# States gathered behind the scores into the banks of values and of y, summed by one running sum out of PSUM, and the share put behind the own values

## The chip, the core and the metric

The kernel runs on one core of a Trainium2 chip. The metric is device time in microseconds: the median of three runs of the kernel before is 128.42 us (127.86 to 129.88).

## What is computed

Eight batches of 512 tokens with 128 features. Each is normalised, goes through retention attention with 8 heads of 16 features in blocks of 64 tokens, and through a feed-forward layer of 512 hidden features with squared relu, whose weights are rounded to -1, 0 and 1 times a scale. Cut to what matters:

```python
qs, ks, vs = map(to_chunks, (q, k, v))          # blocks of 64 tokens
def step(S, x):
    qc, kc, vc = x
    attn = jnp.einsum('bhid,bhjd->bhij', qc, kc) * D
    o_intra = jnp.einsum('bhij,bhje->bhie', attn, vc)
    o_inter = jnp.einsum('bhid,bhde->bhie', qc * decay_q[None, :, :, None], S)
    S_new = decay_s[None, :, None, None] * S + jnp.einsum('bhjd,bhje->bhde', kc * decay_k[None, :, :, None], vc)
    return (S_new, o_intra + o_inter)
...
h = _bitlinear(x, w_fc) + gate * (x @ v.T @ fast_b.T @ u.T)
r = jnp.maximum(h, 0.0)
return _bitlinear(r * r, w_proj)
...
xn = _layernorm(x, axis=-1)
x = x + attention(xn) + ffn(xn)
```

## The kernel before

Everything is written out by hand: each engine has its own program, and semaphores with counts tie them together. The batches go through a prologue (the first batch's projections and hidden layer, and all weights), a loop of three rounds with two bodies each (batches 1 to 6), and a tail for the last batch. A body of index b carries three batches at once: it computes hidden layers and attention of b, finishes b - 1 and normalises and projects b + 1.

Full-width products are split in three terms (`three_terms`, L659, L660, L663) or are single products of 512 columns. The attention is made of small tiles of the 128x128 array:

- `score` (L705): 32 products of 32 rows and 64 columns, into the four banks of `ps_score`. `mask_scores` (L516, DVE) multiplies each bank by the causal mask into `scores`.
- `gather_states` (L720): 28 products of 64 rows and 32 columns, k transposed times v for each block of 64 tokens. They go into two banks of `ps_score` (numbers 2 and 3) and so must wait until the masks of these banks are done.
- `own_values` (L735): 64 products of 64 rows and 32 columns, the part of the output that comes from the tokens of the block itself, into banks 0 and 1.
- `carry` (L747), called the share here: 28 products of 32 rows and 32 columns, the part of the earlier blocks. Its weights are the sums of the states over all blocks before. It adds to the banks of `own_values`. `o_done` then lets ACT round the sum (`high_o`, L360, `o_hi`), and DVE takes what is left (`low_o`, L538, `o_lo`).

The sums of the states take DVE four instructions: `take_states` (L524) masks them into `sums_of[0]`, and `add_states` (L532) adds with distances of 1, 2 and 4 blocks. Each waits for the one before.

In a body TensorE does, in this order: hidden layers 0 and 1, the second product and the share of the batch before, hidden layers 2 and 3, the turn of xn (`turn_xn`, L668, four transposes into `ps_turn`), the scores, the output product of the batch before, q, k and values by token (`project_vk`, two banks, `ps_turn` and `ps_y`), the states and own values. DVE in a body: statistics of b + 1, `take_states` and `add_states` of b - 1 with the variance between them, four steps of the inverse root, normalising (L491, four instructions), `low_o`, `low_xn` (L497), two masks, `finish` (L544), `decay_q` (L501), two masks, `take_v` twice. ACT takes relu, squares (`take_square`) and their rounded copies (`high_square`). POOL subtracts the copies (`low_square`, L300) and spreads q over pairs of heads (`spread_q`, L305).

## Time and profile before

| | us |
|---|---|
| median of three runs | 128.42 |
| profiled execution, its own time | 129.01 |
| its span, first to last instruction | 127.04 |
| TensorE busy | 117.0 |
| DVE busy | 99.2 |
| ACT busy | 78.7 |
| POOL busy | 64.0 |
| prologue, to the first product of the loop | 24.89 |
| bodies of batches 1 to 6 | 15.02, 15.26, then 52.71 for four |
| tail, from the last batch's first product | 19.16 |

The span is what the trace shows, and the execution lasts 1.97 us longer. A row of the timeline has the start, the time from the first to the last instruction of the row, the engine, the line and the shapes. A matmul's end is modelled and lies behind the start of its successor, so distances between starts tell the pace. TensorE takes a product of 32-bit numbers that aren't rounded in two passes, so 28 products are x56 in the trace.

### The profile page before, as it was taken

The numbers are of one execution on the slowest core, as the hardware profiler recorded it, in microseconds if no ns is written. First come the engines' busy times: TensorE is split into PE (matmuls) and PEld (weight loads), VectorE is DVE, ScalarE is ACT, GpSimd is POOL, SyncE is SP. The second block draws the span as 40 slices with busy tenths as digits, with TensorE's granted clock in tenths as the row PEclk, the third lists the DMA queues.
The fourth block names the chain that finished last, engine by engine and source line by source line (L and its number), as shares of the span: only waits on it lengthen the run. The fifth ranks groups of instructions, "written<-read, shape, count | busy, mean of one in ns | idle before, by whom it ended". The sixth has DMA issues, their size and how long they took to land.

```text
span 127.0 us, 6564 instructions
## 1 busy us (share of the span) xinstructions
PE 117.0 (92%) x2860; PEld 92.8 (73%) x2860; DVE 99.2 (78%) x261; ACT 78.7 (62%) x158; POOL 64.0 (50%) x60
## 2 busy tenths in 40 slices
PE   4979999988999999499999999999999999499991
PEld 4425869856688778377788778878897889377890
DVE  0788795489799969858699979896999799729832
ACT  3265669967871897227972897188738774382910
POOL 7099803984439161923439252916193529544400
PEclk9999999999999999999999999999999999999998
DMA  3849920000023000400023001300020002000202
GB/s 105 296 149 320 389 92 34 0 3 5 8 90 81 5 0 23 145 7 0 0 92 74 0 0 53 112 0 0 0 83 0 0 0 83 0 5 0 88 5 83
DMA packets 3357, 7.71 MB, mean 61 GB/s; under 512 B 384, under 2 KB 896, under 8 KB 3216
## 3 DMA queue, kind: packets, MB, share of 16 engines
q1 hardware_dynamic: 2880, 7.01, 16.3%
q10 hardware_dynamic: 464, 0.50, 1.2%
q8 instruction: 11, 0.18, 0.6%
q14 instruction: 2, 0.02, 0.0%
HBM read 5.42 MB, written 2.10 MB: 59 GB/s over the span
## 4 chain that ended last, share of the span: by engine, by line
PE 80%; DVE 10%; issue 4%; ACT 2%; POOL 1%; DVEq 0%; POOLq 0%
PE ps_work L659 10%; PE ps_score L735 8%; PE ps_work L663 7%; PE ps_work L660 7%; PE ps_score L705 6%; PE ps_score L747 5%; PE ps_score L781 5%; PE ps_y L761 4%; PE ps_y L762 4%; PE ps_score L720 3%; DVE sums_of L532 3%; PE ps_turn L668 3%; PE ps_y L765 2%; DVE xn L491 2%; PE ps_turn L692 1%
## 5 line engine op out<-in xcount | busy, mean ns | idle before, releaser
L300 POOL TENSOR_TENSOR sq_lo<-square,sq_hi 128x512 fp32r<-128x512 f32 x31 | 39.8, 1295 | 36.2 <-ACT sq_hi L356 36.2
L347 ACT ACTIVATE square<-ps_work 128x512 f32<-128x512 f32 x32 | 19.1, 596 | 23.1 <-PE ps_work L663 22.6
L516 DVE TENSOR_TENSOR scores<-ps_score,cst 128x512 f32<-128x512 f32 x32 | 20.3, 682 | 1.6 <-PE ps_score L705 1.6
L305 POOL TENSOR_TENSOR q_pair<-q_dec,cst 128x1024 f32<-128x1024 f32 x7 | 13.3, 1894 | 15.9 <-DVE q_dec L501 15.9
L356 ACT ACTIVATE sq_hi<-square 128x512 fp32r<-128x512 f32 x32 | 20.1, 627 | 0.1
L352 ACT ACTIVATE square<-square 128x512 f32<-128x512 f32 x32 | 18.9, 630 | 0.1
L491 DVE TENSOR_SCALAR xn<-x_in,mean_var,rstd 128x128 f32<-128x128 f32 x32 | 14.9, 528 | 0.3
L659 PE MATMUL ps_work<-xn_hi,w_hi 128*128 128x512 f32 x32 | 14.3, 447 | 0.4 <-issue 0.4
L735 PE MATMUL ps_score<-scores,v_pad 64*32 64x64 f32 x1024 | 12.5, 225 | 1.6 <-issue 1.6
L663 PE MATMUL ps_work<-xn_lo,w_hi 128*128 128x512 f32 x32 | 12.6, 394 | 0.0
L660 PE MATMUL ps_work<-xn_hi,w_lo 128*128 128x512 f32 x32 | 12.6, 393 | 0.0
L735 PEld LDWEIGHTS ps_score<-scores,v_pad 64*32 64x32 f32 x1024 | 11.0, 105 | 2.1 <-issue 1.8
L532 DVE TENSOR_TENSOR sums_of<-sums_of 128x224 f32<-128x224 f32 x24 | 12.0, 502 | 0.6
L761 PE MATMUL ps_y<-sq_hi,w 128*128 128x512 f32 x28 | 11.2, 400 | 0.5 <-POOL sq_lo L300 0.5
L762 PE MATMUL ps_y<-sq_lo,w 128*128 128x512 f32 x28 | 11.0, 392 | 0.0
L497 DVE TENSOR_TENSOR xn_lo<-ps_turn,xn_hi 128x512 fp32r<-128x512 f32 x8 | 5.5, 692 | 6.6 <-ACT xn_hi L334 6.6
L458 DVE BATCH_NORM_STATS2 stats<-x_in 128x6 f32<-128x128 f32 x32 | 6.9, 279 | 4.6 <-DMA x_in<-x_tok 4.0
L747 PEld LDWEIGHTS ps_score<-q_dec,sums_of 32*32 32x32 f32 x448 | 6.6, 105 | 4.8 <-issue 4.8
L747 PE MATMUL ps_score<-q_dec,sums_of 32*32 32x64 f32 x448 | 7.9, 216 | 2.1 <-DVE sums_of L532 2.1
L705 PE MATMUL ps_score<-q_pair,k_feat 32*64 32x128 f32 x512 | 9.7, 278 | 0.0
L705 PEld LDWEIGHTS ps_score<-q_pair,k_feat 32*64 32x64 f32 x512 | 7.7, 130 | 1.5 <-DVE o_lo L538 0.9
L659 PEld LDWEIGHTS ps_work<-xn_hi,w_hi 128*128 128x128 f32 x32 | 6.0, 187 | 3.1 <-issue 0.7
(123 smaller groups left out, 238.6 us busy)
## 6 DMA issues: line engine op xcount, KB each, us to landing
x_in<-x_tok SPq DMA_DIRECT2D x8, 256.0 KB, 3.4
resid<-x_feat SPq DMA_DIRECT2D x1, 2048.0 KB, 7.7
out_feat<-resid SPq DMA_DIRECT2D x7, 256.0 KB
po_in<-ffn_weights SPq DMA_DIRECT2D x1, 320.0 KB, 3.2
fc_in<-ffn_weights SPq DMA_DIRECT2D x1, 256.0 KB, 3.7
q_table<-q_decay SPq DMA_DIRECT2D x1, 256.0 KB, 3.5
wqvk<-qvk_weights ACTq DMA_DIRECT2D x1, 192.0 KB, 3.9
cst<-const ACTq DMA_DIRECT2D x1, 129.0 KB, 3.9
```

The costliest lines, as they stand in the source:

```text
L300: nc.gpsimd.tensor_tensor(sq_lo[p][:, f, :], square[p][:, f, :], sq_hi[p][:, f, :].bitcast(F32), ALU.subtract).then_inc(lo_ready, 1)
L347: nc.scalar.activation(square[b.parity][:, f, :], ps_work[f % 2][:], ACT.Relu).then_inc(relu_ready, 1)
L352: nc.scalar.activation(sq, sq, ACT.Square).then_inc(square_ready, 1)
L356: nc.scalar.activation(sq_hi[b.parity][:, f, :], square[b.parity][:, f, :], ACT.Copy).then_inc(hi_ready, 1)
L491: ins = nc.vector.tensor_scalar(xn[:, t, :], x_in[b.parity][:, t, :], mean_var[:, t, 0:1], rstd[:, t:t + 1], ALU.subtract, ALU.mult)
L516: nc.vector.tensor_tensor(scores[:, g].rearrange("p t s i -> p (t s) i"), ps_score[:, g].rearrange("p (a i) -> p a i", i=BLK), causal.unsq ...
L659: mm(out, w_hi, x_hi, start=True, stop=False)
L660: mm(out, w_lo, x_hi, start=False, stop=False)
L663: return mm(out, w_hi, x_lo, start=False, stop=True)
L705: ins = mm(ps_score[r * BLK:(r + 1) * BLK, g, t * P:(t + 1) * P], k_feat[b.parity][rows, toks], q_pair[b.parity][rows, :, toks], start=Tru ...
L735: mm(ps_score[g * GW:(g + 1) * GW, r, t * BLK:(t + 1) * BLK], v_pad[b.parity][rows, t, g, s * GW:(s + 1) * GW], scores[rows, g, t, s, :], ...
L747: ins = mm(ps_score[rows, r, t * BLK:(t + 1) * BLK], sums_of[3][rows, PAD + blk - 1, :], q_dec[b.parity][rows, blk * BLK:(blk + 1) * BLK], ...
```

## The change

The states are gathered right behind the scores, into the first columns of `ps_turn` and `ps_y`, now two halves of one tensor `ps_both`. They don't wait for a mask any more, but the turn of xn, which writes `ps_turn`, waits until `take_states` has read them. `take_states` of batch b now stands in the body of b. It writes the masked states back to PSUM (bank 2 of `ps_score`, whose scores have been masked by then), with the blocks innermost. One instruction on DVE, a running sum (`tensor_tensor_scan`), multiplies by `restart` (0 at the start of each run of 8 blocks, 1 elsewhere) and adds. The share reads its weights out of `state_sums` with a step of 8 elements, and stands behind the own values of the same batch. The second product stands as a whole behind the turn. DVE and ACT work a body ahead on the statistics: the variance of b + 2 is at the end of the body of b, which makes their last bodies stand outside the loop. POOL zeroes no paddings but sets up `restart`, and does all four subtractions before it spreads q. The last of them in the tail has moved from DVE to POOL. The 32-row products that TensorE runs in the prologue to pass the time are now `place_program`: 12, 27 (behind the first turn) and 7 (between own values and share of the first batch), and 22 in the tail in place of 6.

```diff
+        state_sums = sb("state_sums", [P, GW * NBLK])
+        restart = sb("restart", [P, GW * NBLK])
...
+        ps_both = pb("ps_both", [P, ROWS, SEQ])
+        ps_turn, ps_y = ps_both[:, 0, :], ps_both[:, 1, :]
+        w1_bank = ps_score[:, NG - 1, :]
+        masked_states = ps_score[:, ROWS, 0:GW * NBLK]
...
             def take_states(b):
 
+                dve.wait_ge(scores_ready, b.count(NG, 1))
                 dve.wait_ge(state_done, b.count(1, 1))
                 nc.vector.tensor_tensor(
-                    sums_of[0][:, PAD:].rearrange("p (t r) e -> p t r e", r=ROWS),
-                    ps_score[:, ROWS:2 * ROWS, 0:NT * GW].rearrange("p r (t e) -> p t r e", e=GW),
...
-            def add_states(b, k):
-                dve.wait_ge(state_step, b.count(3, k + 1))
...
+                    masked_states.rearrange("p (e t r) -> p r t e", t=NT, r=ROWS),
+                    ps_both[:, :, 0:NT * GW].rearrange("p r (t e) -> p r t e", e=GW),
+                    pair_mask.unsqueeze(1).unsqueeze(1).broadcast_to([P, ROWS, NT, GW]),
+                    ALU.mult).then_inc(states_taken, 1)
+
+            def sum_states(b):
+                dve.wait_ge(states_taken, b.count(1, 1))
+                nc.vector.tensor_tensor_scan(state_sums[:], restart[:], masked_states, 0.0, ALU.mult,
+                                             ALU.add).then_inc(state_ready, 1)
...
-            def turn_xn(b):
+            def turn_xn(b, before=None):
                 pe.wait_ge(xn_ready, b.count(1, 1))
+                if before is not None:
+
+                    pe.wait_ge(states_taken, before.count(1, 1))
...
-                pe.wait_ge(scores_ready, b.count(NG, ROWS))
+                pe.wait_ge(v_ready, b.count(2, 2))
...
-                            ins = mm(ps_score[g * GW:(g + 1) * GW, ROWS + r, t * GW:(t + 1) * GW],
+                            ins = mm(ps_both[g * GW:(g + 1) * GW, r, t * GW:(t + 1) * GW],
...
-                        ins = mm(ps_score[rows, r, t * BLK:(t + 1) * BLK], sums_of[3][rows, PAD + blk - 1, :],
+                        ins = mm(ps_score[rows, r, t * BLK:(t + 1) * BLK], state_sums[rows, blk - 1:GW * NBLK:NBLK],
...
+            def place_program(n, bank, data):
+
+
+                for k in range(n):
+                    rows = slice(k % NG * GW, (k % NG + 1) * GW)
+                    mm(bank[rows, 0:BLK], data[rows, 0:GW], data[rows, 0:BLK], start=True, stop=True,
+                       skip_group_check=True)
...
+            place_program(27, ps_score[:, 0, :], ident)
...
+            own_values(first)
+            place_program(7, ps_score[:, NG - 1, :], ident)
+            carry(first)
+
+            def hidden_and_scores(b):
 
                 pe.wait_ge(q_ready, b.count(1, 1))
                 hidden(b, 0)
                 pe.wait_ge(k_ready, b.count(1, 1))
                 hidden(b, 1)
...
+                pe.wait_ge(o_lo_ready, b.count(1, 0))
+                score(b)
+                gather_states(b)
                 hidden(b, 2)
                 hidden(b, 3)
...
+                turn_xn(after, b)
+                second_product(before, ps_y, range(NF))
                 output_product(before, ps_y)
                 project_q(after, b)
                 project_k(after, b)
                 project_vk(after, 0)
                 project_vk(after, 1)
-                gather_states(b)
                 own_values(b)
+                carry(b)
...
+            hidden_and_scores(last)
+            pe.wait_ge(states_taken, last.count(1, 1))
+            second_product(before, ps_y, range(NF))
             output_product(before, ps_y)
...
+            pe.wait_ge(scores_ready, last.count(NG, NG))
+            pe.wait_ge(state_ready, last.count(1, 1))
+            place_program(22, ps_score[:, NG - 1, :], ident)
             own_values(last)
             carry(last)
...
+            for f in range(NF):
+                last_second(f)
```

On TensorE, in the second body of the loop before (the names stand for tiles without their numbers; REGISTER_ALU and ISA rows set up waits), the share stands between the second product and hidden layer 2:

```order
L761 MATMUL ps_y<-sq_hi,w 128x512
L762 MATMUL ps_y<-sq_lo,w 128x512
L747 MATMUL ps_score<-q_dec,sums_of 32x64 x28
L754 ISA
L659 MATMUL ps_work<-xn_hi,w_hi 128x512
```

In the same body of the changed kernel, scores and states stand there, behind hidden layer 1:

```order
L679 MATMUL ps_work<-xn_hi,w_lo 128x512
L682 MATMUL ps_work<-xn_lo,w_hi 128x512
L719 ISA
L725 MATMUL ps_score<-q_pair,k_feat 64x128 x32
L740 MATMUL ps_both<-v_pad,k_tok 32x32 x28
L774 ISA
L678 MATMUL ps_work<-xn_hi,w_hi 128x512
```

So scores and states have become neighbours ahead of hidden layers 2 and 3, and the turn comes behind both.

At the end of the same body TensorE had, behind the last product of the values by token:

```order
L694 MATMUL ps_y<-wqvk_hi,xn_lo 128x2x128
L720 MATMUL ps_score<-v_pad,k_tok 32x32 x28
L735 MATMUL ps_score<-scores,v_pad 32x64 x64
L83 REGISTER_ALU
L83 COMPARE_AND_BRANCH
```

and has now:

```order
L714 MATMUL ps_both<-wqvk_hi,xn_lo 128x2x128
L755 MATMUL ps_score<-scores,v_pad 32x64 x64
L767 MATMUL ps_score<-q_dec,state_sums 32x64 x28
L83 REGISTER_ALU
L83 COMPARE_AND_BRANCH
```

The share is the last thing that a body does, and its rounding on ACT falls into the next body's first products.

On DVE, in the second body of the loop before, the states of the batch before stood in front of the root and of normalising:

```order
L524 TENSOR_TENSOR sums_of<-ps_score,cst 128x256
L466 BN_AGGR mean_var<-stats 128x2 x4
L468 REGISTER_ALU
L469 TENSOR_SCALAR var_eps<-mean_var 128x4
L531 ISA
L532 TENSOR_TENSOR sums_of<-sums_of 128x224
```

and the states of the batch itself now stand behind normalising (L508) and two masks (L533), with the running sum (L550) further down:

```order
L508 TENSOR_SCALAR xn<-x_in,mean_var,rstd 128x128 x4
L533 TENSOR_TENSOR scores<-ps_score,cst 128x512 x2
L540 ISA
L542 TENSOR_TENSOR ps_score<-ps_both,cst 128x2x4x32
L533 TENSOR_TENSOR scores<-ps_score,cst 128x512 x2
L514 TENSOR_TENSOR xn_lo<-ps_both,xn_hi 128x512
L550 SCALAR_TENSOR_TENSOR state_sums<-restart,ps_score 128x256
```

## Rows read from the trace of the kernel before

**Rows 1.** Stretches: length; PE, PEld, DVE, ACT, POOL busy; clock; DMA share, GB/s

```profile
0.00:24.89 24.89, 22.39 (x352) 15.79 (x352) 15.88 (x56) 15.65 (x34) 14.84 (x25) 1.00 0.50 177
24.89:39.91 15.02, 13.81 (x352) 10.72 (x350) 13.39 (x38) 9.88 (x20) 8.87 (x7) 1.00 0.14 39
39.91:55.17 15.26, 13.43 (x354) 10.98 (x350) 13.48 (x39) 8.98 (x18) 8.33 (x7) 1.00 0.11 38
55.17:68.27 13.10, 13.10 (x350) 10.88 (x350) 9.98 (x25) 8.99 (x18) 5.27 (x4) 1.00 0.14 39
68.27:107.88 39.61, 39.43 (x1053) 32.69 (x1048) 35.64 (x91) 26.96 (x54) 20.89 (x16) 1.00 0.08 27
107.88:127.04 19.16, 14.84 (x418) 11.79 (x415) 10.79 (x17) 8.21 (x14) 5.84 (x5) 0.98 0.09 30
```

**Rows 2.** Timeline, TensorE, fifth body: start, length, line, shapes, count

```profile
84.71 0.40 PE L762 MATMUL ps_y<-sq_lo,w 128*128 128x512 f32 x1
85.03 0.98 PE L747 MATMUL ps_score<-q_dec,sums_of 32*32 32x64 f32 x56
85.95 0.50 PE L659 MATMUL ps_work<-xn_hi,w_hi 128*128 128x512 f32 x1
86.29 0.39 PE L660 MATMUL ps_work<-xn_hi,w_lo 128*128 128x512 f32 x1
86.52 0.39 PE L663 MATMUL ps_work<-xn_lo,w_hi 128*128 128x512 f32 x1
...
87.96 1.21 PE L705 MATMUL ps_score<-q_pair,k_feat 32*64 32x128 f32 x64
89.10 0.50 PE L765 MATMUL ps_y<-o_hi,wo_hi 128*128 128x512 f32 x1
...
92.78 0.69 PE L720 MATMUL ps_score<-v_pad,k_tok 64*32 64x32 f32 x56
93.32 1.47 PE L735 MATMUL ps_score<-scores,v_pad 64*32 64x64 f32 x128
```

**Rows 3.** Timeline, TensorE: second body and tail

```profile
53.97 1.01 PE L735 MATMUL ps_score<-scores,v_pad 64*32 64x64 f32 x77 [1.64 <-issue]
...
110.45 0.98 PE L747 MATMUL ps_score<-q_dec,sums_of 32*32 32x64 f32 x56 [1.61 <-DVE sums_of L532]
...
119.74 1.67 PE L735 MATMUL ps_score<-scores,v_pad 64*32 64x64 f32 x128
121.34 0.98 PE L747 MATMUL ps_score<-q_dec,sums_of 32*32 32x64 f32 x56
...
123.30 0.59 PE L881 MATMUL ps_turn<-o_last,wo_full 128*128 128x256 f32 x2
```

**Rows 4.** Timeline, DVE, fifth body

```profile
81.67 0.42 DVE L524 TENSOR_TENSOR sums_of<-ps_score,cst 128x256 f32<-128x256 f32 x1
...
84.13 0.17 DVE L475 RECIPROCAL rstd<-std 128x4 f32<-128x4 f32 x1
...
84.93 2.09 DVE L491 TENSOR_SCALAR xn<-x_in,mean_var,rstd 128x128 f32<-128x128 f32 x4
...
88.70 0.69 DVE L497 TENSOR_TENSOR xn_lo<-ps_turn,xn_hi 128x512 fp32r<-128x512 f32 x1 [1.08 <-ACT xn_hi L334]
89.31 1.28 DVE L516 TENSOR_TENSOR scores<-ps_score,cst 128x512 f32<-128x512 f32 x2
```

**Rows 5.** Timeline, DVE, prologue

```profile
16.19 1.12 DVE L491 TENSOR_SCALAR xn<-x_in,mean_var,rstd 128x128 f32<-128x128 f32 x4
```

**Rows 6.** Timeline, ACT, fifth body

```profile
86.08 0.60 ACT L360 ACTIVATE o_hi<-ps_score 128x512 fp32r<-128x512 f32 x1 [0.53 <-PE ps_score L747]
```

**Rows 7.** Timeline, POOL, fifth body

```profile
85.63 1.31 POOL L300 TENSOR_TENSOR sq_lo<-square,sq_hi 128x512 fp32r<-128x512 f32 x1 [2.59 <-ACT sq_hi L356]
```

**Rows 8.** Groups of the page: busy us, mean ns, idle before

```profile
L747 PEld LDWEIGHTS ps_score<-q_dec,sums_of 32*32 32x32 f32 x448 | 6.6, 105 | 4.8 <-issue 4.8
...
L705 PEld LDWEIGHTS ps_score<-q_pair,k_feat 32*64 32x64 f32 x512 | 7.7, 130 | 1.5 <-DVE o_lo L538 0.9 <-issue 0.5
```

232 lines of the change are left out of this document (104 added, 128 removed).

## The prediction

> **What bounds the kernel now.** I read the busy time by stretches first, then TensorE's rows of one body, then every stretch in which TensorE stands still. By stretches [rows 1], a body that nothing disturbs takes 13.10 us and TensorE is busy for all 13.10; DVE is busy 9.98 of them, ACT 8.99, POOL 5.27. So between 55 and 108 us TensorE alone sets the time, and what the other engines do there costs nothing as long as it isn't late. The disturbed stretches are the first body (15.02, TensorE busy 13.81), the second (15.26, busy 13.43) and the tail (19.16, busy 14.84). Two stops are seen singly [rows 3]: 1.64 us inside L735 of the second body, released by "issue" alone (no engine is waited for: the instructions themselves were not there), and 1.61 us in the tail, where the share L747 waits for the third DVE addition.
>
> **TensorE's price list** [rows 2]. A full-width product starts 0.23 us after the one before (86.29 to 86.52). The first one behind a group of small tiles holds its successor 0.34 back (85.95 to 86.29), 0.11 more. A small group behind a full-width product starts 0.32 after it (84.71 to 85.03), 0.09 more. Groups by start to start: share 0.92, scores 1.14 (87.96 to 89.10), states 0.54, own values 1.40 (its 1.47 less the 0.07 by which a successor starts early, as 1.21 and 1.14 at the scores). Between two groups of different small shapes the tail has the one case: the share at 121.34 starts 1.60 behind own values at 119.74 [rows 3], where 1.40 is usual; I put 0.13 of the 0.20 down to the change of shape and the rest to the same thin supply of instructions as in the second body.
>
> **The steady body.** Its matrix work is the same before and after. Before, it enters small tiles three times (share; scores; states with own values); after, twice (scores with states; own values with share): 0.09 + 0.11 = 0.20 saved. But two groups of different small shapes now touch twice: 2 x 0.13 = 0.26 added. That gives 13.10 - 0.20 + 0.26 = 13.16 us if nobody is late: no gain. The Trainium skill's page "TensorEngine Tiling (Array Packing)", Tiling Modes, says that changing the tiling mode drains the engine. By that rule each touch costs something; a trade of three entries for two without the touches would give 12.90.
>
> Who could be late? The turn of xn, which now waits for states_taken. I lay out DVE's chain from the start S of the body's first product. The share before ends at S + 0.07; o_hi starts 0.07 later and takes 0.60 [rows 6]; o_lo starts at 0.77. Its successor starts 0.61 later, as behind L497 at 88.70 [rows 4]: 1.38. The four root steps take 0.80 (84.13 to 84.93): 2.18. Normalising took 2.09 at 84.93 but 1.12 at 16.19 [rows 5]; in the first case a POOL subtraction of 1.31 us ran from 85.63 [rows 7], and one of the four instructions was stretched. With POOL idle its successor starts 1.03 later: 3.21. Two masks, 1.20 (of 1.28 for the pair): 4.41. The masking of the states, 0.42 (L524): 4.83, plus 0.05 of signalling: 4.88. TensorE is at the turn at S + 1.49 (two triples, 0.34 + 5 x 0.23) + 0.09 + 1.14 + 0.13 + 0.54 + 1.49 = 4.88. The two meet to the hundredth. o_lo itself ends at 1.45 and the scores want it at 1.58. POOL's first subtraction starts at 3.56 (relu 0 from 1.01, relu 1 from 1.70, square 2.19, its copy 2.85 to 3.48, 0.08 of signalling; each takes 0.60 to 0.65 as o_hi does, an estimate from rows of the same width [rows 6]), 0.27 after normalising has ended. So the wait is hidden, with no margin.
>
> DVE's other edits have cover. The scan replaces three additions (1.23 us together). No row shows a scan: below, it takes as long as one pass of 256 elements (0.42, L524); above, as long as the three additions, 1.23. I take 0.6. It ends near S + 7.4, and the share needs it at 12.3, so either end costs nothing. By the Trainium skill, "DVE: opcode table, instruction layouts, handler registers and perf-mode slots", Datapath and trigger behaviour, the built-in scan runs at half throughput; that speaks for a value between the ends and changes nothing in the sum. Behind the scan stand finish and the q table, ready at S + 8.9 and 9.5; the second values bank wants the first at 10.0.
>
> Six bodies, then: 6 x 13.16 = 79.0, plus 0.2 at each of two loop branches (39.61 is 0.31 over three times 13.10, with one branch in it), 79.4. Before, the same six took 15.02 + 15.26 + 13.10 + 39.61 = 82.99. **Term one: -3.6 us**, and all of it is stops that go away. In body 1 before, the share waited for additions that stood behind the statistics of the next batch; now all of that is done in the prologue.
>
> **The head.** Added: the first batch's own share, 0.91 + 0.13; 27 placeholder products, whose 54 passes at the share's rate (0.92 / 56 = 0.0164) take 0.89 where TensorE waited about 0.8 anyway, so 0.1; 7 more before the share, 0.23; another change of shape, 0.13. Without the states and own values between the turn and q, q waits for xn_hi and xn_lo: 0.60 + 0.60 + 0.69 from the turn's start [rows 4, 6] plus a relu that stands ahead, against about 1.3 of cover (eight transposes and two terms of q): 0.75. The second values bank waits for wo_lo, behind a mask, the scan, the q table and wo_lo itself (0.60 + 0.6 + 0.60 + 0.3) against 1.7 of cover (seven full-width products and a half bank): 0.3. Off: about 0.3 of waits between scores and hidden layers. **Term two: +2.2 us** (24.89 becomes 27.1).
>
> **The tail**, from the last batch's first product: 4.88 to the turn's place (no turn, and no normalising, so the states are masked by 4.4), 11 full-width products 2.53: 7.41; 0.09 + 22 placeholders 0.72: 8.22; shape 0.13, own values 1.40, shape 0.13, share 0.92: 10.80; 0.11 + 16 half-width products at 0.116 (before, eight of them fill 122.26 to 123.30 less 0.11): 12.8; then as before from 123.30 to the end of the span at 127.04, 3.74: 16.5. The last lo tile is ready at 10.1 and o_last at 11.3, both early. **Term three: 16.5 - 19.16 = -2.7 us**: 1.6 of it is the wait for the additions, the rest is the share of the batch before, which has moved ahead.
>
> **Supply of instructions.** The stop of 1.64 us fell into a run of 92 small products. The changed kernel has such runs in the head (99 with the placeholders), in each body (own values and share, 92) and at the end (114), and 62 more small products ahead of the loop, so everything lies elsewhere in the code. From below: no stop. From above: three of 1.64 (head, first pass, tail), 4.9 us. The nearest row shows one stop in four such runs passed for the first time. I take half a stop: **+0.8 us**.
>
> Sum: -3.6 + 2.2 - 2.7 + 0.8 = -3.3 us on the profiled span of 127.04. That execution lasted 129.01, 1.97 outside the span, which the change doesn't touch. Against the median 128.42: **125.1 us**.
>
> **Rivals.** *Slower: DVE's chain meets POOL.* The turn has no margin, and the 0.27 us between the end of normalising and POOL's first subtraction is all that keeps them apart. In the kernel before they do overlap, and it costs 2.09 - 1.12 = 0.97 per body. If the chain slips by more than 0.27 (a slower state mask doesn't count, it stands behind), every body gains up to 0.97: 125.1 + 6 x 0.97 = 130.9. For it: the collision is there in every body now. Against: POOL's start is fixed by relu 0 and relu 1 behind o_hi, and slips with the same o_hi. 10%.
>
> *Spread layouts cost.* The share's weights are now read with a step of 8 elements and the states are written to PSUM with that step. No row shows a stepped operand. Lower bound nothing. Upper bound for the weights: 14 loads in a row per share, each longer by the 25 ns by which a load of twice the columns is longer (130 ns at L705, 105 at L747) [rows 8], 0.35 us; the states' mask, if half again as long, 0.2 at the turn. 7 or 8 times 0.35 to 0.55: +2.6 to +4.2, 127.7 to 129.3. The Trainium skill, "SBUF — State Buffer", Door 1: The DMA port swizzle, says that steps over a 16-byte line cost bandwidth, and that PSUM's lines have 8 bytes; by that rule this rival is what happens, at the price just given. What covers it: loads overlap products. 18%.
>
> *Instructions come late two or three times.* +1.64 each beyond the half: 127.5 to 129.2. For it: longer dense runs than before. Against: TensorE's later passes of the loop show none. 17%.
>
> *The change moves nothing but stops and these were chance* (the 1.9 us over 13.10 in the first body come back): 127. 5%.
>
> **Chances and range.** My forecast 50%. About 2% (below 125.9 or above 131.0) is what a measurement of this kernel can tell from no change. Faster by over 2%: nine tenths of the forecast (its own range reaches past 125.9) and the part of the code rival with one whole stop, 0.50. Slower: 0.10. Within 2%: 0.40. Low end: no stop, some touches free (6 bodies at 12.98): 123.3. High end 128.8 leaves out the POOL rival and the worst of the others. The forecast's own range is 123.3 to 126.3.
>
> **What would show it.** Body stretches of 13.1 to 13.3 by TensorE's rows; the wait of the turn for the states below 0.2; normalising near 1.1, not 2.1; the scan between 0.42 and 1.23; the share still 0.92 (if the weights' step costs, it shows there); the tail 16.5 from the last batch's first product; "issue" waits summed. I am wrong if the bodies differ from 13.16 by more than 0.3, or if the head ends far from 27.

## The result, and the profile after

The changed kernel takes 131.39 us in the median of four runs (130.80 to 133.15); beside it the kernel before took 128.79 (127.86 to 129.88). The ratio is 1.021, with an interval of 1.011 to 1.031. So it is slower, by 1 to 3%, where 125.1 was forecast, and outside the range of 123.3 to 128.8. Medians also hold executions in which TensorE's clock fell for a while (last section), so the comparisons below are made on profiled spans: 128.8 us, against 127.0 before and the 123.8 that the sum gave.

The profiled execution by stages, cut at the first product of each body and of the last batch (columns as in [rows 1]):

```profile
0.00:28.67 28.67, 24.14 (x476) 16.97 (x476) 19.44 (x68) 16.88 (x36) 18.34 (x26) 1.00 0.45 154
28.67:43.74 15.07, 13.36 (x351) 11.12 (x349) 10.24 (x30) 9.72 (x19) 6.93 (x5) 1.00 0.15 39
43.74:58.08 14.34, 13.57 (x356) 11.11 (x350) 10.08 (x29) 9.61 (x18) 6.96 (x5) 1.00 0.12 40
58.08:71.23 13.15, 13.15 (x349) 10.97 (x349) 10.06 (x29) 9.54 (x18) 6.95 (x5) 1.00 0.16 40
71.23:111.04 39.81, 39.78 (x1054) 32.90 (x1048) 28.72 (x78) 28.60 (x53) 20.85 (x15) 1.00 0.08 27
111.04:128.80 17.76, 13.93 (x396) 11.31 (x391) 6.19 (x11) 7.87 (x14) 5.07 (x4) 1.00 0.10 32
```

The undisturbed body is 13.15, as forecast. Against the forecast the head is 1.57 longer (28.67 for 27.1), the six bodies 2.97 (82.37 for 79.4) and the tail 1.26 (17.76 for 16.5); less the 0.8 that the sum held for the supply of instructions, that is the 5.0 by which the span missed. The median missed by 6.3; nearly all of the rest is that the profiled execution was 0.6 above its median before and is 0.6 below it now. The timeline of TensorE has four stretches in which it stands still and is released by "issue", where before there was one large one [rows 3]:

```profile
28.40 0.34 PE L767 MATMUL ps_score<-q_dec,state_sums 32*32 32x64 f32 x3 [1.19 <-issue]
...
33.83 0.25 PE L740 MATMUL ps_both<-v_pad,k_tok 64*32 64x32 f32 x4 [1.69 <-issue]
...
56.59 0.41 PE L755 MATMUL ps_score<-scores,v_pad 64*32 64x64 f32 x19 [0.72 <-issue]
...
121.83 0.32 PE L755 MATMUL ps_score<-scores,v_pad 64*32 64x64 f32 x10 [1.16 <-issue]
```

They sum to 4.76 us. An x in these rows counts passes, two for a product, so the stops stand three passes before the end of the first share, four before the end of the states of batch 1, 19 before the end of the own values of batch 2, and ten before the end of the tail's own values. Each lies inside a group of equal small products, where nothing in the program waits. In the chain of the page, issue has 4% of the span.

The steady body, DVE and TensorE, fourth body (timeline):

```profile
71.37 0.60 ACT L372 ACTIVATE o_hi<-ps_score 128x512 fp32r<-128x512 f32 x1 [0.65 <-PE ps_score L767]
72.00 0.69 DVE L555 TENSOR_TENSOR o_lo<-ps_score,o_hi 128x512 fp32r<-128x512 f32 x1 [1.52 <-ACT o_hi L372]
72.61 0.17 DVE L492 RECIPROCAL rstd<-std 128x4 f32<-128x4 f32 x1
...
72.83 1.21 PE L725 MATMUL ps_score<-q_pair,k_feat 32*64 32x128 f32 x64
...
73.40 1.12 DVE L508 TENSOR_SCALAR xn<-x_in,mean_var,rstd 128x128 f32<-128x128 f32 x4
...
73.97 0.69 PE L740 MATMUL ps_both<-v_pad,k_tok 64*32 64x32 f32 x56
...
74.59 0.51 PE L678 MATMUL ps_work<-xn_hi,w_hi 128*128 128x512 f32 x1
...
74.80 1.30 POOL L314 TENSOR_TENSOR sq_lo<-square,sq_hi 128x512 fp32r<-128x512 f32 x1 [4.35 <-ACT sq_hi L368]
...
75.63 0.42 DVE L542 TENSOR_TENSOR ps_score<-ps_both,cst 128x256 f32<-128x256 f32 x1
...
76.20 0.63 PE L690 MATMUL ps_both<-cst,xn 128*128 128x128 f32 x4
```

### The profile page after: what moved, and what is told of

It is laid out like the page before. It is cut to its first block, busy times and chain, and to the rows that moved or that the text cites. A ratio compares the mean times of both kernels' runs of the same rounds, so it can differ in the third digit from the quotient of the medians.

```text
span 128.8 us, 6716 instructions
## 1 busy us (share of the span) xinstructions
PE 117.9 (92%) x2960; PEld 94.4 (73%) x2960; DVE 84.7 (66%) x244; ACT 82.2 (64%) x158; POOL 65.1 (51%) x60
## 4 chain that ended last, share of the span: by engine, by line
PE 87%; issue 4%; DVE 4%; DMA 3%; ACT 1%
PE ps_work L678 11%; PE ps_score L755 9%; PE ps_work L682 9%; PE ps_work L679 9%; PE ps_score L725 7%; PE ps_score L767 6%; PE ps_both L781 5%; PE ps_both L782 5%; PE ps_both L740 4%; PE ps_both L712 3%; PE ps_both L690 3%; PE ps_both L713 3%; PE ps_both L714 3%; DMA x_in<-x_tok 3%; PE ps_score L801 2%
## 5 line engine op out<-in xcount | busy, mean ns | idle before, releaser
L314 POOL TENSOR_TENSOR sq_lo<-square,sq_hi 128x512 fp32r<-128x512 f32 x32 | 40.8, 1293 | 51.6 <-ACT sq_hi L368 51.6
L533 DVE TENSOR_TENSOR scores<-ps_score,cst 128x512 f32<-128x512 f32 x32 | 20.6, 681 | 1.4 <-PE ps_score L725 1.4
L364 ACT ACTIVATE square<-square 128x512 f32<-128x512 f32 x32 | 19.8, 620 | 0.0
L555 DVE TENSOR_TENSOR o_lo<-ps_score,o_hi 128x512 fp32r<-128x512 f32 x7 | 4.8, 691 | 11.6 <-ACT o_hi L372 11.6
L781 PE MATMUL ps_both<-sq_hi,w 128*128 128x512 f32 x28 | 11.5, 410 | 0.0
L524 DVE TENSOR_TENSOR v_pad<-ps_both,cst 128x256 f32<-128x256 f32 x16 | 6.7, 424 | 6.9 <-ACT k_tok L354 6.8
L782 PE MATMUL ps_both<-sq_lo,w 128*128 128x512 f32 x28 | 11.0, 392 | 0.0
L767 PE MATMUL ps_score<-q_dec,state_sums 32*32 32x64 f32 x448 | 9.1, 223 | 1.2 <-issue 1.2
L767 PEld LDWEIGHTS ps_score<-q_dec,state_sums 32*32 32x32 f32 x448 | 7.8, 141 | 2.0 <-issue 1.3
L508 DVE TENSOR_SCALAR xn<-x_in,mean_var,rstd 128x128 f32<-128x128 f32 x32 | 8.9, 342 | 0.3
L712 PE MATMUL ps_both<-wqvk_hi,xn_hi 128*128 128x256 f32 x32 | 9.0, 283 | 0.0
```

Source lines behind the costliest of these rows:

```text
L314: nc.gpsimd.tensor_tensor(sq_lo[p][:, f, :], square[p][:, f, :], sq_hi[p][:, f, :].bitcast(F32), ALU.subtract).then_inc(lo_ready, 1)
L364: nc.scalar.activation(sq, sq, ACT.Square).then_inc(square_ready, 1)
L533: nc.vector.tensor_tensor(scores[:, g].rearrange("p t s i -> p (t s) i"), ps_score[:, g].rearrange("p (a i) -> p a i", i=BLK), causal.unsq ...
L767: ins = mm(ps_score[rows, r, t * BLK:(t + 1) * BLK], state_sums[rows, blk - 1:GW * NBLK:NBLK], q_dec[b.parity][rows, blk * BLK:(blk + 1) * ...
L781: mm(bank[:], w2[:, f, :], sq_hi[b.parity][:, f, :], start=(f == 0), stop=False)
```

## The experiments

**What the stops look like in the trace.** The page counts 12 packets of the queue of kind "instruction" with 0.20 MB. Each is a transfer of 16,384 bytes, and the trace has its start and end. I counted TensorE's instructions in the program (two for a pass, its weight load and its product, and one each for a wait or a register operation) and looked up at which one it went on after each stop. In this table the places modulo 256 and the last column are the telling ones:

```
kernel         instruction after the stop   transfer (us)    goes on   behind its end
before             1984  (192 mod 256)      51.65 to 52.61    53.97      1.36
changed             958  (190)              26.14 to 27.08    28.40      1.32
changed            1215  (191)              31.37 to 32.45    33.83      1.38
changed            2239  (191)              54.00 to 55.43    56.59      1.16
changed            3007  (191)              119.61 to 120.56  121.83     1.27
```

All five places are 190 to 192 behind a multiple of 256, in two programs whose loops start 250 instructions apart. Between 58.76 and 114.08 us, while the loop runs on, the changed kernel's trace has no such transfer on that queue. That gave **theory A, late code**: TensorE's code comes in blocks of 256 instructions; in these five cases the transfer of the next began some 40 to 110 passes ahead of its edge, and TensorE went on 2.2 to 2.6 us after it began (up to 3.2 in the runs below). Wide products (0.23 us a pass) fill that time; small ones (0.010 to 0.018 us a pass) don't, so an edge behind a long run of small ones is a stop. The loop's code stays once it has been passed, so only head, first pass and tail pay. The Trainium skill has the blocks: by "Runtime: NRT & Kernel Launch", Instruction fetch mechanics, code is refilled in blocks of 16 KiB, 256 instructions, and TensorE holds 2,048. The trace agrees as far as it goes: transfers of 16,384 bytes, places 256 apart, and a loop of 1,426 instructions that isn't fetched again. The same section says that this fetching is hidden, because dispatch is slower than the fill. The traces contradict that for small products. The rivals: **B**, the stops belong to the new work at those places; **C**, chance.

**20 placeholders at the start in place of 27.** The seven lay in time in which TensorE waits anyway; all later code moves 28 instructions towards the start.

```diff
-            place_program(27, ps_score[:, 0, :], ident)
+            place_program(20, ps_score[:, 0, :], ident)
```

> The changed kernel with 20 placeholders in place of 27 in the wait for the rounded x of batch 0; those 7 lay in time in which TensorE waits, so no work on the path goes away, and the 7 ahead of the first share stay. Every later instruction of TensorE stands 28 places earlier in its code. Theory A (late code: TensorE's instructions come in blocks of 16 KB, which are 256 instructions; a transfer takes about 1 us, TensorE goes on 1.3 us behind its end, and the edges of blocks that follow 50 passes of small products are caught waiting): the edges at instruction 961 and 1217, now at 28.40 and 33.83, fall 14 passes later in the stream, behind the wide products of layer one; both stops (1.19 and 1.69 us) go or shrink below 0.8, the one in batch 2 (0.72) may grow to 1.3 and move from the middle of the own values, the one in the tail (1.16) stays within 0.3. Net -1.2 to -2.8 us against the changed kernel: 128.6 to 130.2. Theory B (the stops belong to the new work at these places, the wait for the first scan and the first states, or to the memory traffic at that time): no change over 0.3 us, stops stay at the end of the first share and in the states of batch 1. Theory C (chance): stops appear elsewhere without order.

Measured: 133.62 us, ratio to before 1.039 (1.019 to 1.059), span 131.4. Where the two stops had been there is none; the one in batch 2 is 1.20 and five passes from the end of its group in place of 19; the 14 passes between are the 28 instructions. That is as A has it, to the place (a small one of 0.30 us came up in the states of batch 0, at 18.37). The time is not: 128.6 to 130.2 was expected. Batch 2 starts at 43.59, where it started at 43.74, so the two stops that went gave 0.15; its own stop cost 0.5 us more, and the last stage took 20.0 us for 17.76, because its stop was 1.77, not within 0.3 of 1.16, and the clock fell behind it (last section). Why the first two gave nothing is in the timeline of this kernel:

```profile
27.24 1.90 POOL L319 TENSOR_TENSOR q_pair<-q_dec,cst 128x1024 f32<-128x1024 f32 x1
...
28.22 0.94 DVE L486 TENSOR_SCALAR var_eps<-mean_var 128x4 f32<-128x4 f32 x1
...
29.20 0.21 ACT L342 ACTIVATE std<-var_eps 128x4 f32<-128x4 f32 x1 [2.71 <-DVE var_eps L486]
29.37 0.60 ACT L372 ACTIVATE o_hi<-ps_score 128x512 fp32r<-128x512 f32 x1
...
30.83 1.48 PE L725 MATMUL ps_score<-q_pair,k_feat 32*64 32x128 f32 x64 [1.58 <-DVE o_lo L555]
...
31.41 2.15 DVE L508 TENSOR_SCALAR xn<-x_in,mean_var,rstd 128x128 f32<-128x128 f32 x4
...
35.24 0.66 PE L690 MATMUL ps_both<-cst,xn 128*128 128x128 f32 x4 [0.71 <-DVE ps_score L542]
```

The share of batch 0 ended 1.1 us earlier, at 27.60, but o of batch 0 was rounded only at 29.37, because ACT's root stands ahead of it and waits for the variance of batch 2, and that takes 0.94 us (0.39 to 0.48 in the loop) while POOL spreads q. The scores waited 1.58 us for it. Now DVE was late for the whole body: normalising met POOL's first subtraction (2.15 for 1.12), and the turn waited 0.71 for the states. So there is a second bound at the same place, hidden behind the stop. In the changed kernel:

```profile
26.76 1.90 POOL L319 TENSOR_TENSOR q_pair<-q_dec,cst 128x1024 f32<-128x1024 f32 x1
...
27.74 0.94 DVE L486 TENSOR_SCALAR var_eps<-mean_var 128x4 f32<-128x4 f32 x1
...
28.72 0.20 ACT L342 ACTIVATE std<-var_eps 128x4 f32<-128x4 f32 x1 [2.72 <-DVE var_eps L486]
28.89 0.60 ACT L372 ACTIVATE o_hi<-ps_score 128x512 fp32r<-128x512 f32 x1
...
30.35 1.20 PE L725 MATMUL ps_score<-q_pair,k_feat 32*64 32x128 f32 x64
```

**The same code places, less work.** 34 placeholders at the start, the seven ahead of the first share out.

> The changed kernel without the 7 placeholders ahead of the first share, with 34 in place of 27 at the start, where TensorE waits. Later instructions stand where they stood in the code, the work on the path is less by 7 small products (0.25 us). Theory A (late code): the stops stay at the same instructions and about as long as before, sum 4.5 to 5.5 us; time 131.0 to 131.8. Theory B (the placeholders or what stands there cause the stop at the end of the first share): that stop goes, -1.2 us or more.

Measured: 133.44 us, ratio 1.033 (1.013 to 1.052), profiled span 131.8. The stops are at the very same passes, the end of the first share less three, the own values of batch 2 less 19, the tail's less ten: 1.80, 1.00 and 1.71 us. Against B: the placeholders next to the first share were gone and the stop stayed. The one in the states of batch 1 is not shown as idle, but the first of the states starts at 33.47 and the group lasts 1.04 where 0.69 is usual. The time is 2 us over what A expected (131.0 to 131.8). The granted clock fell twice in the profiled execution, which the last section shows; the one execution of the four with a mean clock of 1.00 took 131.9.

**The kernel before with 15 placeholders more**, 60 instructions, in a wait of 0.78 us behind the first turn.

```diff
             turn_xn(first)
+            for k in range(15):
+                rows = slice(k % NG * GW, (k % NG + 1) * GW)
+                mm(ps_score[rows, 0, 0:BLK], ident[rows, 0:GW], ident[rows, 0:BLK], start=True, stop=True,
+                   skip_group_check=True)
             pe.wait_ge(wqvk_split, 1)
```

> The kernel before with 15 placeholders (30 passes, 60 instructions) behind the turn of batch 0, in the 0.78 us that TensorE waits there for the rounded x; 27 of them took 0.98 us in the changed kernel, so 15 fit into the wait (0.55 us) and cost nothing by themselves. Theory A (late code): the edges of blocks fall elsewhere: the stop at 53.97 (1.64 us, own values of batch 2) goes, new ones come near 22 (own values of batch 0, up to 2.2 us), near 42 (1.5 to 2.1 us) and in the tail near 125 (1.5 to 2.4 us); the sum rises from 1.6 to 4.5 to 6.6 us and the kernel takes 131.5 to 133.5 us. Theory B (the changed kernel's stops belong to its new order of work): the kernel before stays at 128.8 +- 0.3, with its one stop in batch 2.

Measured: 135.23 us, ratio 1.058 (1.042 to 1.075), at a profiled span of 132.2 with full clock. Its stops:

```profile
24.11 0.35 PE L735 MATMUL ps_score<-scores,v_pad 64*32 64x64 f32 x16 [1.93 <-issue]
...
44.55 0.32 PE L735 MATMUL ps_score<-scores,v_pad 64*32 64x64 f32 x9 [2.45 <-issue]
...
127.14 0.30 PE L747 MATMUL ps_score<-q_dec,sums_of 32*32 32x64 f32 x3 [1.87 <-issue]
```

The stop at 53.97 [rows 3] is gone and three others came, near 22, 42 and 125 as forecast; TensorE goes on at instructions 702, 1471 and 3007 (190, 191, 191 mod 256), 1.43 to 1.47 us behind the end of the transfer. The three sum to 6.25 us, inside the 4.5 to 6.6 expected; the time is 1.7 over the 133.5 that A allowed, and even the execution at full clock took 134.18. Nothing of the change is in this kernel. So B falls, and so does C: by the profiled spans (132.2 and 127.0) fifteen tiny products that lie in a wait cost the kernel before 5.1 us, 4.6 of it by stops, because of where they push the code.

**Weights of the share in one piece.** The share then multiplies by other values; this kernel is there for the price of the step alone.

```diff
-state_sums[rows, blk - 1:GW * NBLK:NBLK]
+state_sums[rows, (blk - 1) * GW:blk * GW]
```

> The changed kernel with the share's weights read as 32 neighbouring words of the summed states, not with a step of 8 words (other values are read, so the output is not the reference's; sizes, waits and code length are the same). Theory 'spread weights cost': the share takes 0.91 to 0.93 us from start to start in place of 1.02, the mean weight load of the share 105 ns in place of 141, and the kernel 0.8 us less (8 x 0.10): 130.6. Theory 'the 0.10 is the step from tiles of 64 rows to tiles of 32 ahead of the share': the share stays at 1.02 and the time at 131.4 +- 0.2. In both the four stops stay.

Measured: 130.68 us, ratio 1.022 (1.006 to 1.039), span 128.5. The group of the share's weight loads, first in the changed kernel, then in this one (busy, mean ns):

```profile
L767 PEld LDWEIGHTS ps_score<-q_dec,state_sums 32*32 32x32 f32 x448 | 7.8, 141 | 2.0 <-issue 1.3
```

```profile
L767 PEld LDWEIGHTS ps_score<-q_dec,state_sums 32*32 32x32 f32 x448 | 6.8, 105 | 2.4 <-issue 1.7
```

And the share, from its start to that of the next group, 0.92 (69.87 to 70.79) for 1.02 (70.21 to 71.23). The step of 8 costs 36 ns a load, 0.10 us a share, 0.8 in all; the change of shape ahead of the share costs nothing. The medians can't confirm that: 130.68 is 0.7 under the changed kernel's 131.39, but the two ranges overlap. The spans differ by 0.3, with stops of 1.55, 1.40, 0.72 and 1.61 us in this one, 0.5 more in sum, which leaves the same 0.8.

**The second bound taken away.** DVE's statistics and variance of batch 2, once, ahead of the values of batch 1, where DVE waited 2.19 us; with 27 placeholders, then with 20.

```diff
+            statistics(first.step(2))
+            statistics_done(first.step(2))
+            variance(first.step(2))
             take_v(after, 0)
             take_v(after, 1)
-            statistics(first.step(2))
-            statistics_done(first.step(2))
-            variance(first.step(2))
```

> The changed kernel with the statistics and the variance of batch 2, once, ahead of the values of batch 1 in VectorE's code, where VectorE waits 2.19 us for TensorE. Same code on TensorE. In the changed kernel the variance takes 0.94 us at 27.74 (GpSimd runs the spread from 26.76 to 28.66), the root on ScalarE waits for it and the rounding of o of batch 0 stands behind the root (28.89), so the scores of batch 1 start at 30.35. Theory 'two bounds at one place' (the stop of 1.2 to 1.8 us at the end of the first share and this chain end within 0.3 us of each other, so taking away either alone gives almost nothing): the stop stays, the rounding of o starts 0.05 us behind the share, the scores start right behind layer one; gain 0.1 to 0.3 us. Theory 'the chain sets the head': gain over 1 us.

> The same edit and 20 placeholders in place of 27 at the start, so that the edges of the code's blocks fall 14 passes later in the stream. Theory 'two bounds at one place': no stop at the end of the first share and none in the states of batch 1, and now no wait for o either: scores of batch 1 start 1.2 to 1.9 us earlier than with 20 alone (30.83), at 28.9 to 29.6, and batch 2 starts at 41.5 to 42.3 (43.59 with 20 alone, 43.74 in the changed kernel). The stops in batch 2 and in the tail stay. A profile without a fall of the clock has a span of 126.3 to 127.3 us (128.8 in the changed kernel). Theory 'late code alone' (the first edit does nothing): as with 20 alone.

Measured with 27: 133.19 us, ratio 1.041 (1.031 to 1.051), span 129.3. The stop stays (1.00, until 28.10), the scores start at 29.95, 0.40 earlier than in the changed kernel, and the first body still ends at 43.36. TensorE's code is that of the changed kernel, and the stops stand at the same passes, but they last 1.00, 1.66, 1.24 and 1.43 us for 1.19, 1.69, 0.72 and 1.16. So the length of one stop scatters by up to half a microsecond while its place stays. With 20 as well: 130.42 us, ratio 1.020 (1.010 to 1.029), span 127.7:

```profile
27.67 0.60 ACT L372 ACTIVATE o_hi<-ps_score 128x512 fp32r<-128x512 f32 x1 [1.34 <-PE ps_score L767]
...
29.12 1.64 PE L725 MATMUL ps_score<-q_pair,k_feat 32*64 32x128 f32 x64
...
54.92 0.31 PE L755 MATMUL ps_score<-scores,v_pad 64*32 64x64 f32 x5 [1.19 <-issue]
...
120.97 1.08 PE L767 MATMUL ps_score<-q_dec,state_sums 32*32 32x64 f32 x52 [1.73 <-issue]
```

The four kernels make a square. Batch 2 starts at 43.74 with neither edit, at 43.59 with the placement alone, at 43.36 with the statistics alone, and at 41.46 with both: 0.15 and 0.38 alone, 2.28 together. Two bounds stood at one place. These are single executions: the kernel of the next but one experiment has TensorE's code of the last of the four up to that point, and starts batch 2 at 41.07. Against 2.28 such a scatter of 0.4 is small, against 0.15 and 0.38 it isn't. The span did not reach the 126.3 to 127.3 that I expected, since the stops in batch 2 and in the tail grew by 0.5 and 0.6.

**The tail.** The 22 placeholders out, two tiles of the last second product in their place; then the same with both edits above, with the seven placeholders moved rather than the 27 cut.

```diff
-            place_program(22, ps_score[:, NG - 1, :], ident)
-            own_values(last)
-            carry(last)
             pe.wait_ge(relu_ready, last.count(NF, 3))
-            for f in range(NF):
+            last_second(0)
+            last_second(1)
+            own_values(last)
+            carry(last)
+            for f in range(2, NF):
                 last_second(f)
```

> The changed kernel with the 22 placeholders ahead of the last own values taken out and the second products of the first two tiles of the last batch put there (they stood behind the last share). Theory: the 22 placeholders (0.79 us from 118.49 to 119.28) cover no wait, since the sums of the states were there at 117.27 and the masked scores at 116.7; the tail gets 0.7 to 0.8 us shorter, minus what the low part of the second tile is late. The stop in the tail moves in the stream (72 instructions fewer ahead of it) to the share or near its start and stays 1.0 to 1.9 us: it depends only on 50 passes of small products ahead of an edge, and own values and share are 184 passes in a row. Rival: the wide products ahead give the code time, and the stop goes (-2 us in all). Other stops unchanged.

> Statistics of batch 2 early, the tail's second products first, and the 7 placeholders ahead of the first share out (27 stay at the start). Theory: no stop at the end of the first share and none or under 0.5 us in batch 1, scores of batch 1 at 28.9 to 29.3; a stop in batch 2 (1.0 to 1.4 us) and one in the tail (1.0 to 1.9 us) stay; span 125.0 to 126.5 without a fall of the clock, against 128.8 of the changed kernel and 125.4 to 127.0 of the kernel before. Rival: the new order of work costs more in the steady bodies than it gives, then nothing here brings it below 128.

Measured: 133.08 us, ratio 1.034 (1.026 to 1.042), and 130.87 us, 1.022 (1.012 to 1.033). The profiled spans are 131.6 (with a fall of the clock in batch 3) and 127.5, where 125.0 to 126.5 was expected. The placeholders covered nothing, but the tail's stop moved to the share and grew to 2.16 and 2.01 us, over the 1.9 that I allowed, and took the 0.8 back: the last stage lasts 17.97 and 17.88 us, for 17.76. The second kernel has the same code places in the loop as the one before it in this list (20 and 7 placeholders against 27 and 0), yet a stop of 1.02 at 40.11 that the other lacks, and that I had put at under 0.5: its transfer began at 37.23 for 36.24, though its body had begun 0.5 earlier. When a transfer begins isn't fixed by the distance to the edge: over all these runs it lay between 0 and 126 passes ahead, and for the stop of 2.45 us above it began only when TensorE stood still (42.16). What sets it stays open; perhaps how TensorE waited before. So A gives the places, not each length.

**Wide products between the small ones.** Early statistics, 20 placeholders, the tail's 22 out, and two tiles of the second product between own values and share:

```diff
-            place_program(22, ps_score[:, NG - 1, :], ident)
-            own_values(last)
-            carry(last)
             pe.wait_ge(relu_ready, last.count(NF, 3))
-            for f in range(NF):
+            own_values(last)
+            last_second(0)
+            last_second(1)
+            carry(last)
+            for f in range(2, NF):
                 last_second(f)
```

> The changed kernel with the statistics of batch 2 early, 20 placeholders at the start, the tail's 22 placeholders out, and the second products of the last batch's first two tiles between its own values and its share (8 passes of 256 columns, 0.92 us). Theory (a run of small products over 100 instructions long ahead of an edge leaves the code late; wide products in between give it time): up to batch 6 as with the first two edits alone (batch 1 ends at 41.5, one stop of 1.2 us in the own values of batch 2, last stage starts at 109.3); the stop in the tail falls from 1.75 us to 0.4 to 1.0; with the 0.8 us of the placeholders the tail is 1.6 to 2.1 us shorter, the span 125.6 to 126.1 without a fall of the clock, and the kernel level with the kernel before within 1%. Rival (the tail's stop depends on the transfer alone): it stays over 1.5 us, span 126.9.

Measured: 127.66 us over six runs, beside 128.72 of the kernel before; ratio 0.997 (0.992 to 1.002), level with it. The profiled span is 126.1:

```profile
27.75:41.07 13.32, 13.32 (x355) 11.17 (x350) 10.08 (x29) 9.54 (x18) 8.32 (x6) 1.00 0.15 44
41.07:55.91 14.84, 13.60 (x354) 11.12 (x350) 10.05 (x29) 9.60 (x18) 6.96 (x5) 1.00 0.12 39
...
108.91:126.10 17.19, 13.35 (x353) 10.69 (x347) 6.19 (x11) 7.87 (x14) 5.08 (x4) 0.98 0.10 32
```

The first body runs in 13.32 with TensorE busy throughout. What is left in the tail:

```profile
120.87 0.47 PE L767 MATMUL ps_score<-q_dec,state_sums 32*32 32x64 f32 x16 [1.08 <-issue]
```

The tail's stop fell to 1.08 us (0.4 to 1.0 was expected), and the tail is 1.26 shorter than with the first two edits alone (18.45), not 1.6. The low ratio is no gain of the change alone: this kernel has three edits more, and the kernel before kept its own stop of 1.64.

**Values and k between own values and share in the loop**, on top of that:

```diff
                 project_k(after, b)
+                own_values(b)
                 project_vk(after, 0)
                 project_vk(after, 1)
-                own_values(b)
                 carry(b)
```

> The same, and in the loop the projection of values and k by token (12 passes of 256 columns, 1.36 us) between own values and share in place of ahead of the own values. Theory: the 368 instructions of small products in a row are cut into 256 and 112, so the share is never caught waiting; whether the stop in batch 2 stays depends on its edge falling over 100 instructions into the own values (it stood 5 products from their end, so with the projection behind it stays near 1.0 to 1.3, or moves). Each body pays two more changes of the tile's shape, 0.1 to 0.2 us, 0.7 to 1.4 us in all, so the kernel gets slower by up to 1 us against the run without this edit. Rival: changes of shape cost nothing and the values taken later hold the turn (VectorE reaches the low part of o late): bodies longer by 0.4 us or more.

Measured: 131.09 us, ratio 1.024 (1.016 to 1.031). The rival holds as well as the theory, and the kernel is 3.4 us slower than the one without this edit, where up to 1 was expected. No stop of 0.3 us or more is left in the loop, the body of batch 2 included, and the tail's is 0.61. But each of the last three bodies of the loop lasts 13.8 to 13.9 us for 13.2 to 13.4, and there the scores wait:

```profile
71.63 0.69 DVE L555 TENSOR_TENSOR o_lo<-ps_score,o_hi 128x512 fp32r<-128x512 f32 x1 [0.76 <-ACT o_hi L372]
...
72.45 1.20 PE L725 MATMUL ps_score<-q_pair,k_feat 32*64 32x128 f32 x64 [0.35 <-DVE o_lo L555]
```

The values are taken so late that the variance, the root and with them o are late. The wait is 0.35; by the prices of [rows 2], 0.11 and 0.09, the one more change to small products and back is an estimated 0.20. Stops paid once were traded for 0.6 us in every body. One body of this run shows more, batch 3 with 15.06 us:

```profile
56.11 0.60 ACT L372 ACTIVATE o_hi<-ps_score 128x512 fp32r<-128x512 f32 x1 [0.22 <-issue]
...
58.13 2.17 DVE L508 TENSOR_SCALAR xn<-x_in,mean_var,rstd 128x128 f32<-128x128 f32 x4
...
58.94 1.28 POOL L314 TENSOR_TENSOR sq_lo<-square,sq_hi 128x512 fp32r<-128x512 f32 x1 [4.68 <-ACT sq_hi L368]
...
61.99 0.63 PE L690 MATMUL ps_both<-cst,xn 128*128 128x128 f32 x4 [0.78 <-DVE ps_score L542]
```

There ACT's instructions were late by 0.22 us on top. Normalising was still running when POOL's subtraction began, took 2.17 in place of 1.12, and the turn waited 0.78 for the states.

## Why the prediction was wrong, point by point

**The steady body** was right: 13.15 for 13.16. DVE's chain came within 0.01 us at each station: the successor of o_lo 1.38 behind the body's start (1.38 forecast), normalising at 2.17 (2.18), the masks at 3.20 (3.21), the states' mask at 4.40 (4.41), 0.28 between normalising and POOL (0.27). In detail the sum held by errors that cancel. The two touches of small shapes were put at 0.13 each and cost nothing (72.83 to 73.97 is 1.14, as in [rows 2]; own values to share is 1.41). The states take 0.62 to the wide product behind them (73.97 to 74.59), 0.08 more than the 0.54 of [rows 2]. The share takes 0.10 more by its weights, and the turn starts at 4.97, 0.10 late: the states' mask ends at 76.05 and the turn follows 0.15 later, not the 0.05 of my sum. The tail's odd 0.20 in [rows 3] was mostly no change of shape: inside those own values one pass, at 120.72, starts 0.12 behind the one before it in place of 0.01. It stands at an edge of the code (194 mod 256 by the trace's records), 1.31 us behind the end of a transfer (118.35 to 119.41). The Trainium skill's rule on draining at a change of tiling mode ("TensorEngine Tiling (Array Packing)", Tiling Modes) has no measurable price here between two small shapes.

**DVE meets POOL** (10%) did not happen in the steady bodies: normalising took 1.12 in each. It did in two bodies of the experiments in which DVE was late for another reason (2.15 and 2.17 us), as that rival put it: its place and its price were right, and the margin of 0.28 us was enough. The Trainium skill ("SBUF — State Buffer", Who interferes with whom) calls the pair of ports that the two share an exclusive lock; the traces agree in part, see the last section.

**Spread layouts** (18%) were a tenth of a microsecond per share, not 0.35 (and 7 or 8 times 0.35 to 0.55 is 2.5 to 4.4, not 2.6 to 4.2), and the mask to PSUM with that step takes the same 0.42 us as the one before [rows 4]. By the Trainium skill ("SBUF — State Buffer", Door 1) a step over a 16-byte line costs bandwidth; the weight loads agree, 141 ns for 105, but most of it lies under the products. The **scan** took 0.68 us, inside its bounds, and nobody waited for it.

**Head and tail without their stops** were 27.48 and 16.6, for 27.1 and 16.5.

**The supply of instructions** is the step that failed, "I take half a stop". The stops sum to 4.76 us in place of 0.8, close to the top of the bounds (0 to 4.9) that the same paragraph gave. As idle time that is 3.96 of the 5.0 by which the span missed. The other 1.0 is 0.4 in the head and 0.1 in the tail, as just given, and 0.6 in the bodies, which without their stops are 79.96 for 79.4. The sentence "the nearest row shows one stop in four such runs passed for the first time" took the places as a lottery, and the rival "Instructions come late two or three times" had 17% and ended at 129.2. They came late four times. Places in code are not a lottery: the program fixes them. The stop of [rows 3] at instruction 1984 and the 16,384 bytes of a transfer, in the trace of the kernel before, would have given the edges, and counting the changed program's instructions the places at which an edge falls deep into small products. The Trainium skill's page "Runtime: NRT & Kernel Launch" has the 256 too. That "later passes of the loop show none" was right and speaks only for those.

**A step that was missing** is the chain in the first body: variance of batch 2 behind POOL's spread, root, rounding of o. The layout of DVE's chain was made for a steady body and "o_hi starts 0.07 later" was carried over to the first one, where o_hi starts at 28.89. Alone it costs 1.6 us (with 20 placeholders the scores start at 30.83, and layer one is done at 29.25). In the changed kernel it hides under the first stop, so the two are not added; that is why taking the stop away gave nothing.

So the change keeps what it gives, the 1.6 us of waiting for the additions in the tail and the waits of the first body before (0.47 us for POOL and 0.53 for the additions), and loses it in the head's extra work, in code that comes late and in the chain of the first body. The stops alone would not explain it. Two of the four, 2.88 us, stand where that chain holds TensorE nearly as long, and taking them away gave 0.15; only the other two, 1.88 us, stand by themselves. An estimate from the spans: without any stop the changed kernel would be at 126.8 (128.8 less 0.15, 0.72 and 1.16), the kernel before at 125.4 (127.0 less 1.64), and the changed kernel with the early statistics at 124.8 (127.7 less 1.19 and 1.73). No run is free of stops, so whether the order of work by itself is faster isn't shown. That late code makes the stops is shown for their places, by kernels in which only placeholders inside a wait moved the code. That the late code and the chain together make the gap to the forecast is shown to about 1 us, the part that the sum above leaves outside the stops. The nearest run, with head, first body and tail put right, took 127.66, still 2.6 over the forecast, with stops of 0.32, 1.19 and 1.08 us left in it. Whether any placement has no stop at all without longer bodies stays open: own values and share are 368 instructions in a row, so some edge always falls more than 100 deep into them in each body's first pass.

## What to carry to other kernels

When "issue" ends a wait inside a group of equal small products, look for the instruction queue's transfers and count instructions: the stop is a property of the program's layout, and an edit anywhere ahead of it, even one that costs nothing, moves all later ones. Before timing an edit of such a kernel, count where the block edges fall in it and in the kernel before, or the comparison measures the placement (5 us of span here for 15 idle products). And take away a stop only after looking for what is ready just behind it.

## What the runs showed of the hardware that I had not expected

**TensorE's clock can fall behind a stop.** In the kernel with 34 placeholders the profile gives, in stretches of 1 us (PE, PEld, DVE, ACT, POOL, then the granted clock):

```profile
28.00:29.00 1.00, 0.06 (x2) 0.06 (x2) 0.82 (x1) 0.15 (x1) 0.79 (x1) 1.00 0.00 0
29.00:30.00 1.00, 1.00 (x5) 0.84 (x5) 0.06 (x1) 0.65 (x2) 0.00 (x0) 0.62 0.00 0
30.00:31.00 1.00, 1.00 (x3) 0.77 (x3) 0.93 (x4) 0.13 (x1) 0.00 (x0) 0.50 0.00 0
...
33.00:34.00 1.00, 1.00 (x84) 0.83 (x72) 0.42 (x1) 0.97 (x3) 0.00 (x0) 1.00 0.00 0
```

The stop ended at 28.94; from about 29.3 to 32.7 the granted clock was 0.50, that is 1.2 in place of 2.4 GHz, and the wide products of layer one started 0.43 us apart in place of 0.23. The same came behind the tail's stop of that kernel (1.71 us, then 0.50 from 125 to 128) and of the one with 20 placeholders (1.77 us, 0.50 from 124 to 127), and behind the stop of 1.54 us in batch 2 of the kernel with the second products first (0.50 from 60 to 63). Not each stop does it, and its length doesn't decide: behind 2.45 us in the kernel before with 15 more, and behind 1.96 and 2.16 in the kernel with the second products first, the clock stayed at 1.00. I put the cost of a fall at 1.5 us on top, an estimate from the 3.4 us at 0.43 in place of 0.23 a pass. Whole executions with a mean clock of 0.97 to 0.99 were 1 to 5 us longer than those at 1.00, in the kernel before too. That stops make such executions more frequent would fit, but isn't shown. In the last but one experiment, with two stops of about 1.1 us, all six executions had 0.997 or more.

**A variance of 128 x 4 elements waits for GpSimd to finish.** It takes 0.17 us (84.53 in the last kernel) and 0.94 when POOL spreads q at that time. The same holds in the loop, where it takes 0.39 to 0.48 and each time ends 0.02 to 0.03 us behind the spread. In the changed kernel POOL's spread ends at 26.76 + 1.90 = 28.66 and the variance at 27.74 + 0.94 = 28.68; with 20 placeholders 29.14 and 29.16. So it isn't slowed, it is held until the other has ended, and the shortest instruction on DVE bounded the first body. It isn't so for every instruction of POOL. In the prologue of the changed kernel the same variance ran wholly inside a TENSOR_SCALAR instruction of POOL (until 14.3) and took its 0.17, and the other traces have the same:

```profile
12.74 1.59 POOL L307 TENSOR_SCALAR proj_below<-po_in,neg_half 128x512 f32<-128x512 f32 x1
...
13.50 0.17 DVE L486 TENSOR_SCALAR var_eps<-mean_var 128x4 f32<-128x4 f32 x1
```

So the holding is seen against TENSOR_TENSOR on POOL only.
